# K and Q computed with tokens as rows and turned to head rows on VectorE, in place of a trip through HBM, with a new opening

## What is computed

```python
Q = (layernorm(x) @ Wq.T + bq).reshape(bs, sl, H, HD)      # H = 16, HD = 32
K = (ctx @ Wk.T + bk).reshape(bs, sl, H, HD)
V = (ctx @ Wv.T + bv).reshape(bs, sl, H, HD)
score = jnp.einsum('bshd,bsgd->bshg', Q, K)
weight = jax.nn.softmax(score, axis=-1)
attn = jnp.einsum('bshg,bsgd->bshd', weight, V).reshape(bs, sl, nf)
x = x + tanh(g_xattn[0]) * (attn @ Wo.T + bo)
x = x + tanh(g_ffn[0]) * (layernorm(x) @ (weight * scale_weight[:, None]).T + bias)
```

## Time and profile before

| | us |
|---|---|
| median of 3 runs | 281.89 |
| lowest, highest | 281.75, 282.75 |
| span of the profiled execution | 280.1 |
| TensorE busy in it | 267.5 (96%) |
| VectorE busy | 198.8 (71%) |
| ScalarE busy | 144.5 (52%) |
| GpSimd busy | 88.4 (32%) |
| DMA moved | 53.8 MB |

### The profile page before, as it was taken

How to read it: one execution, slowest core, us unless ns; L and a number is a source line. 1 busy time by engine, 2 the same in 40 slices (tenths; PEclk the granted TensorE clock), 3 DMA queues, 4 the chain that set the end, 5 groups by cost and what they waited for, 6 DMA issues and landing times.

```text
span 280.1 us, 8653 instructions
## 1 busy us (share of the span) xinstructions
PE 267.5 (96%) x3516; PEld 235.9 (84%) x3516; DVE 198.8 (71%) x331; ACT 144.5 (52%) x276; POOL 88.4 (32%) x80
## 2 busy tenths in 40 slices
PE   7899998498999999999999999999999999999995
PEld 7789997397978898888988899889988998887775
DVE  2775569189885987569774987579773855598884
ACT  4755543853686236643387225933289432954700
POOL 4104000032157116422183024612183031802722
PEclk9999999899999999999999999999999999999999
DMA  6997769991887764894488853986478729263203
GB/s 204 351 382 226 208 247 249 258 232 56 274 248 237 147 225 150 235 220 139 160 232 247 191 195 130 240 225 156 181 201 246 158 77 231 74 128 72 104 37 112
DMA packets 71912, 53.83 MB, mean 192 GB/s; under 512 B 36688, under 2 KB 59984, under 8 KB 71888
## 3 DMA queue, kind: packets, MB, share of 16 engines
q1 hardware_dynamic: 71744, 52.97, 65.6%
q10 hardware_dynamic: 144, 0.52, 0.5%
HBM read 34.08 MB, written 19.40 MB: 191 GB/s over the span
## 4 chain that ended last, share of the span: by engine, by line
PE 69%; DMA 10%; SPq 7%; ACT 7%; DVE 3%; issue 3%; DVEq 0%; ACTq 0%
PE acc L496 55%; PE score_ps L496 4%; PE score_ps L616 3%; DMA raw_spare<-wq_t 3%; ACT late L796 3%; PE attn_ps L638 3%; PE turn_ps L530 2%; DMA v_scratch<-v_or_norm 2%; SPq L350 2%; DMA k_rows<-k_scratch 2%; DMA q_pad<-q_scratch 2%; SPq L398 1%; SPq L335 1%; DVE turned L1002 1%; DMA q_scratch<-q_t 1%
## 5 line engine op out<-in xcount | busy, mean ns | idle before, releaser
L796 ACT ACTIVATE late<-attn_ps 32x256 f32<-32x256 f32 x124 | 46.6, 376 | 6.1 <-PE attn_ps L638 3.2
L496 PE MATMUL acc<-ctx_parts,wk_parts 128*128 128x256 f32 x384 | 48.7, 285 | 0.3 <-DVE late L1079 0.2
L496 PEld LDWEIGHTS acc<-ctx_parts,wk_parts 128*128 128x128 f32 x384 | 47.1, 191 | 1.7 <-issue 0.8
L1242 POOL TENSOR_TENSOR rstd<-var_eps,minus_half 128x1 f32<-128x1 f32 (+1 forms) x24 | 17.5, 728 | 95.3 <-DVE var_eps L937 95.3
L496 PE MATMUL acc<-wv_parts,ctx_parts 128*128 128x512 f32 x192 | 46.0, 394 | 0.8 <-ACT wv_parts L720 0.8
L496 PEld LDWEIGHTS acc<-wv_parts,ctx_parts 128*128 128x128 f32 x192 | 35.4, 188 | 8.1 <-issue 1.0
L496 PE MATMUL acc<-xa_parts,wq_parts 128*128 128x256 f32 x336 | 41.1, 281 | 0.1
L496 PE MATMUL acc<-wo_parts,xa_parts 128*128 128x512 f32 x168 | 40.4, 395 | 0.6 <-ACT xa_parts L720 0.6
L496 PEld LDWEIGHTS acc<-xa_parts,wq_parts 128*128 128x128 f32 x336 | 40.2, 188 | 0.7 <-DVE xa_parts L913 0.5
L496 PEld LDWEIGHTS acc<-wo_parts,xa_parts 128*128 128x128 f32 x168 | 31.0, 188 | 7.9 <-ACT xa_parts L720 1.0
L496 PE MATMUL acc<-wf_parts,x_parts 128*128 128x512 f32 (+1 forms) x132 | 29.7, 380 | 0.1
(11 more groups left out here) (89 smaller groups left out, 377.7 us busy)
## 6 DMA issues: line engine op xcount, KB each, us to landing
ctx_raw<-ctx_t SPq DMA_DIRECT2D x8, 512.0 KB, 4.7
x_norm<-x SPq DMA_DIRECT2D x8, 512.0 KB, 5.2
k_scratch<-k_t SPq DMA_DIRECT2D x8, 512.0 KB, 3.7
k_rows<-k_scratch SPq DMA_DIRECT2D x32, 128.0 KB, 3.4
q_pad<-q_scratch SPq DMA_DIRECT2D x32, 128.0 KB, 3.2
v_scratch<-v_or_norm SPq DMA_DIRECT2D x32, 128.0 KB, 2.2
v_keys<-v_scratch SPq DMA_DIRECT2D x16, 256.0 KB, 4.3
x_res<-x SPq DMA_DIRECT2D x8, 512.0 KB, 3.8
```

What stands on the lines that cost most here:

```text
L496: last = pe.matmul(dst, left(a, k), right(b, k), start=(n == 0), stop=(n == len(terms) - 1))
L796: nc.scalar.activation(attn_rows(t, q), attn_block(t, q), ACT.Identity).then_inc(a_out, 1)
L1242: nc.gpsimd.tensor_tensor(rstd[which][:, t], var_eps[which][:, t], minus_half[:, t], ALU.pow).then_inc(n_rstd[which], count)
```

## The change

K and Q become layers with tokens as rows (`rows_layer`, 24 matmuls of 512 columns each), one tile in each `acc` bank. VectorE takes each tile out with a block transpose (32x32 blocks) that gives head rows at once: `k_turn(c, t)` to `k_t`, `q_turn(c, t)` to `q_t`. It then adds the biases, `k_bias(c)` writing `k_keys` and `q_bias(c)` in place. ScalarE writes `q_pad` from `q_t` in two instructions with a scale of 0 or 1 per partition (`q_pads`). The scratch tensors of K and Q in HBM, their four kinds of DMA, `cols_bias` and `lay_keys` are gone. The biases come in as eight small DMAs.

The order of tokens in a group changes with the layout: each of the four groups of `attn_ps` now holds tokens of both tiles. `attn_high(c, 0)` therefore waits for all 16 copies, and both `attn_high` stand behind the second lot of copies. V is written to HBM in one DMA where there were four.

In `product` the order of the passes is HI·HI, LO·HI, HI·LO; before it was HI·HI, HI·LO, LO·HI, so that the low part of the left operand is now needed after 4 matmuls and not after 8.

In the opening the context and Wk come in smaller pieces split by feature block, `first_layer` runs K(0), V(0) and Q(0) piece by piece over both tiles, into `acc`, `attn_ps` and `score_ps`; the warm-up has 8 matmuls (`WARM`), before it had 12; the context of chunk 1 has a buffer of its own (`spare_parts`); the transposes of x for chunk 2 stand in step 1 and not at the end of step 0.

On the last chunk the copies are split between ScalarE and VectorE by group, with half as many columns each (`last_attn_copy`).

```diff
-V_SAVED = 4 * DMA
-WARM = (12,)
+V_SAVED = DMA
+WARM = (8,)
...
+                terms = [(k, a, b) for a, b in ((HI, HI), (LO, HI), (HI, LO)) for k in range(KC)]
...
+            def q_layer(c, prev="k", prev_c=None):
+                pe.wait_ge(x1_lo, TILES * (c + 1))
+                rows_layer(x1_parts(c), "wq", q_mm, lambda t: bank_free(prev, c if prev_c is None else prev_c, t))
...
-            k_layer(0, None, 0)
-            v_layer(0, "k", lambda: turn_x1(0, lambda t: None))
-            q_layer(0, "v", 0, WQ)
-            k_layer(1, "q", 0, (0,))
+            first_k_layer()
+            first_layer(WV, ctx_parts, v_mm, lambda t: v_bank(0, t))
+            turn_x1(0, lambda t: None)
+            first_q_layer()
+            k_layer(1, "k", 0, (0,))
             turn_x1(1, x1_read(0))
-            k_layer(1, "q", 0, (1,))
-            q_layer(1, blocks=(0,))
+            k_layer(1, "k", 0, (1,))
...
                 elif first(i - 1):
                     k_layer(2, "v", 1)
+                    turn_x1(2, x1_read(1))
...
-                if first(i):
-                    turn_x1(i + 2, x1_read(i + 1))
...
+                for slot in range(PAD):
+                    nc.scalar.activation(q_pad[:, slot], q_t[:], ACT.Identity, scale=own_slot[:, slot:slot + 1]
+                                         ).then_inc(q_padded, 1)
...
-                    act.wait_ge(a_out, MOVES * c + MOVES // TILES * (tile + 1))
+                    act.wait_ge(a_out, MOVES * (c + 1))
...
-                else:
-                    x1_high(i + 1)
-                    k_bias(i + 1)
+                x1_high(i + 1)
...
-                    q_bias(i + 1)
-                attn_copy(i, 0)
+                attn_copy(i, (0, 1))
                 x2_high(i - 1)
-                attn_high(i, 0)
-                lay_keys(i + 1)
+                q_pads(i + 1)
                 if exists(i + 2):
                     ctx_high(i + 2)
-                attn_copy(i, 1)
+                attn_copy(i, (2, 3))
+                attn_high(i, 0)
                 attn_high(i, 1)
...
+            def k_turn(c, t):
+                dve.wait_ge(k_mm, TILES * c + t + 1)
+                nc.vector.transpose(k_t[:, :, HD * t:HD * (t + 1)], acc[t][:].rearrange("p (h d) -> p h d", d=HD)
+                                    ).then_inc(k_turned, 1)
...
+                nc.vector.tensor_tensor(
+                    k_keys[:], k_t[:].rearrange("p g (n s) -> p n g s", s=2),
+                    bk_keys[:].unsqueeze(1).unsqueeze(3).broadcast_to([P, GT // 2, H, 2]), ALU.add).then_inc(k_laid, 1)
...
+                nc.vector.tensor_tensor(q_t[:], q_t[:], bq_heads[:].unsqueeze(3).broadcast_to([P, QH, KC, GT]),
+                                        ALU.add).then_inc(q_biased, 1)
...
                 spread_first(i)
+                k_turn(i + 1, 1)
+                second_stats(i - 1, 0)
+                k_bias(i + 1)
+                q_turn(i + 1, 0)
+                second_apply(i - 1, 0)
+                second_stats(i - 1, 1)
...
+                second_apply(i - 1, 1)
+                q_turn(i + 1, 1)
+                q_bias(i + 1)
...
+                v_bias(i + 1, 0)
                 turned_lo(x2_parts, x2_hi, x2_lo, i - 1)
-                v_bias(i + 1, 0)
+                attn_low(i, 0)
                 v_bias(i + 1, 1)
-                attn_low(i, 0)
                 f_residual(i - 1, 0)
                 f_residual(i - 1, 1)
                 attn_low(i, 1)
```

511 lines of the change are left out of this document (247 added, 264 removed).

## The result

The changed kernel takes 319.44 us (median of 4 runs, 315.25 to 322.16), the kernel before 282.16 on the same chip (4 runs, 281.75 to 282.75). The ratio is 1.121 with a 95% interval of 1.115 to 1.127: clearly slower. (The ratio rests on the two shorter runs; what is known of why two are longer by 5 us is told with d4.) The profiled execution is the shortest, 315.25 us, with a span of 313.2. The forecast was 299.7 with a range of 290 to 310: right in direction and in the wait that it named, too small in size.

The account below looks back on a forecast made before the run. TensorE, busy 96% of the span, was taken as the bound. Opening -7.6, step 1 +4.75, loop +17.2, step 6 -0.9, end +3.0 and clock +1.3 sum to +17.8: span 297.9, time 299.7 us, range 290 to 310.

Parts of the forecast that it names:

- the wait that it named: Loop, TensorE: F's second tile waits some 3.7 us for v_bias(i+1, 1), through a 6.5 us chain from V's end.
- The clock: Half speed behind the loop's waits: one fall at 1.3 us in the sum, bounds none and one each step, 5.4.
- in the loop no wait for a DMA stands on TensorE's path: Loop: the claim by which removing the scratch traffic, a third of the DMA bytes, was said to bring nothing.
- The opening: Before score(1): waits of 4.16 and 0.92 us go, score(1) starts at 45.8, -7.6 us; bounds -5.1 and -9.
- step 1: From score(1) to score(2): 39.2 us for 34.45, +4.75, from moved transposes and VectorE's added work, with no clock fall.
- 36.4: Length of a loop step in us, score to score; four make 145.6 against 128.4 before, +17.2.
- rival (a): Loop: the clock falls in every step, giving 303.8 us; chance 0.18.
- T+21.0 for the norm: VectorE, loop: the second norm's second application is done 21.0 us after the step's score starts; TensorE wants it at T+20.1.
- k_bias: VectorE: adding K's bias takes 1.15 us, upper bound 2.06, which would raise the sum by 4 x 0.9 us.
- Rival (b): Loop: VectorE is the bound, k_bias at 2.06 and additions slowed beside GpSimd, 305 to 312 us; chance 0.12.
- Steps 6 to 8: Program's end: step 6 -0.9 us, at 26.1; then +3.0 from late norm, late transposes and 16 half-size copies at 4.8.
- rival (c): Loop: the chain behind V's end is hidden and TensorE waits for nothing, 277.6 us; chance 0.05.

Follow-up runs that it names:

- d4: Changed kernel with 10 small matmuls in step 1's 2.6 us wait ahead of V(2)'s second tile on TensorE; 317.2 us.
- a1: Changed kernel with v_bias(i+1, 1) put back ahead of attn_low(i, 0) on VectorE; 307.1 us, ratio 1.091.
- e1: Changed kernel with 12 small matmuls in the wait between F's tiles and save_y(i-1) ahead of load_v(i+1) on SyncE; 311.6 us, ratio 1.105.
- d1: b3 with the loop's context low part on VectorE, f_residual(i-1, 0) ahead of attn_low(i, 0), and step 1 and last-chunk edits; 281.8 us, ratio 1.0046.
- b3: b2 with more reordering on VectorE and SyncE in the loop, and in step 1 and the opening; 294.4 us, ratio 1.045.
- a3: Changed kernel with 12 small matmuls keeping TensorE at work in the wait between the two tiles of F; 315.5 us.
- a4: Changed kernel with save_y(i-1) moved between save_v(i+1) and load_v(i+1) on SyncE; 318.7 us (2 runs).
- c1: Kernel before, with only attn_high(i, 0) moved later on ScalarE and attn_low(i, 0) put ahead of v_bias(i+1, 1) on VectorE; 310.1 us, ratio 1.101.
- b2: b1 with one more wait on GpSimd: x2_bias(i-1) starts only when x1_apply(i+2) is done; 293.6 us, ratio 1.042.
- a2: Changed kernel with ScalarE's second lot of copies and both high parts ahead of ctx_high(i+2); 309.5 us.
- d2: b2 with whole copies on the last chunk (12 on ScalarE, 4 on VectorE) and v_bias(7, 0) ahead of attn_low(6, 0); 293.5 us.
- d3: b2 with the passes of product in their old order, HI*HI, HI*LO, LO*HI; 292.8 us.
- b1: Changed kernel with v_bias(i+1, 1) ahead of attn_low(i, 0) and save_y(i-1) ahead of load_v(i+1); 295.1 us, ratio 1.046.

## Why the prediction was wrong in size

The wait and its chain were right; three terms of the sum were not. The clock was priced as one fall at 1.3 us in the loop and cost 4.6 there. SyncE's queue was put at nothing, by the sentence that no wait for a DMA stands on TensorE's path, and cost 2.6. The opening and step 1 were sized too small, by 6.9 together. The parts in turn:

**The loop (7.3 of the 15.3 us).** One step that failed is the sentence that "in the loop no wait for a DMA stands on TensorE's path", so that SyncE's queue was left out of the sum. It holds for the kernel before. But the change also moved `save_y` behind `load_v`, past a wait for V in HBM, and the instruction list of SyncE was not priced: 2.6 us in steps 2 and 3, and in a1 a second loop of waits of 37.4 us. The larger step is the clock: one fall was in the sum at 1.3; the profile has a half-speed stretch in four of the five steps from 1 to 5, and in the three of them that are in the loop F's second tile takes 1.2 to 1.6 us more, 4.6 with the slower scores behind it. The last 1.4 are what e1's steps have over 36.4: 2.91 us from the start of F's second tile to the next score for 2.75, and a first step of 36.93. So rival (a), 303.8 with 0.18, was the true one as to the clock, and its reason against (3.7 is shorter than 4.16) was wrong: waits of 3.2 were enough, mostly. The first loop of waits itself, 6.5 us behind V's end, T+21.0 for the norm, F's second tile at T+33.7 (measured T+33.8), came out as worked out. e1, with both causes taken out, has steps of 36.7 for the 36.4 of the forecast.

**VectorE's share.** k_bias was put at 1.15 by the nearest row and measured at 1.23; the upper bound came from ScalarE's `lay_keys`, which isn't the same regrouping: it reads every element alone, k_bias two at a time. The Trainium skill ("SBUF — State Buffer", section "Door 1: The DMA port swizzle") asks for two hits on a line of 16 bytes for full bandwidth, and k_bias makes two, so the page doesn't put it near the upper bound, as the prediction has it. The trace agrees with the page: 1.23 us for 1024 elements read eight bytes at a time is no more than the 1.22 of a low part read in a row. Rival (b), VectorE as the bound, is refuted by d1. Its mechanism, instructions slowed beside GpSimd, is real: q_bias 2.24 for 1.22. It costs where the next thing is wanted: 2.1 us in the long form of step 1, 0.8 in b3's steps, but nothing for the 0.33 that F's first tile waits.

**The opening (3.8).** Q(0) ended at 26.46 for the forecast 25.1: two waits of 0.74 and 0.77 us for the parts of x1. "VectorE, through with its queue of step 0 at about 44 (q_bias, k_bias), just keeps up" failed: k_bias(1) ends at 48.3. V(1) waits 1.12 and 0.20 us for `q_turn(1, ·)`, and score(1) 0.49 for `q_pad`. Half of that lateness is one row, the low part of Wo's second half beside GpSimd's `ctx_low(2)`:

```profile
30.52 1.18 DVE L852 TENSOR_TENSOR wo_parts<-spread,wo_parts 128x1024 fp32r<-128x1024 f32 x1
...
34.55 3.38 DVE L852 TENSOR_TENSOR wo_parts<-spread,wo_parts 128x1024 fp32r<-128x1024 f32 x1
```

It takes 3.38 us where the first half took 1.18. GpSimd's `ctx_low(2)` runs from 34.45 to 36.85. b3 moves the low part away from it and `q_bias(1)` ahead of spread, and score(1) comes at 47.3, 2.3 us earlier; no run separates the two moves. The rest is Q(0).

**Step 1 (3.1).** The forecast's 39.2 came from a timetable that the prediction doesn't show; the terms that it names add to 38.3, or 39.6 with the 1.3 for the chain. It puts V's end some 9.3 us before the next score, at T+29.9; it was at 82.2, T+32.6. The added transposes and additions were priced, but V's second tile waits 2.59 us for `q_turn(2, 1)`, later in VectorE's queue than my timetable had it, and 0.85 us are a gap inside score(1) that no row of before shows. "The clock has no reason to fall" was wrong too, though in this run it cost little: F's first tile ran at half speed while its second had to wait for the chain anyway. In the profiled runs of a3, a4 and e1, with the fall one tile earlier, step 1 is 5 us longer, and that is likely most of what lies between the profiled 315.25 and the median of 319.44.

**Steps 6 to 8 (1.2).** Step 6 as forecast, 26.2. Behind it +4.1 for +3.0: waits are where the prediction has them, O(6) 0.59 (it waits for `v_bias(7, 0)`, which stands behind the 16 copies), the transposes of chunk 6 0.57, O(7) 0.84 + 1.51 where 0.57 stood, 2.9 us together; the other 1.2 are a second wait of the transposes, 0.29, and gaps that I can't name. The 16 copies took 5.1 us (forecast 4.8).

**The bounds.** The range ended at 310 because it took the clock from none to one fall a step at 1.3 and no second chain at all. With the clock at its upper bound the sum was 303.8. The 15.6 us from there to the median are the opening 3.8, step 1 3.1, steps 6 to 8 1.1, the rest of the loop 3.2, and the 4.4 between the profiled execution and the median. Two small slips of the prediction change nothing: four falls at 1.3 are 5.2 and not 5.4, and "faster" and "same" have 0.06 together where rival (c), from which they come, has 0.05.

## What to carry to other kernels

A wait that the change adds hides other chains of nearly the same length, and removing it alone then gives back little: list every loop of waits through a step, SyncE's queue among them, and compare their lengths with the step, not only the one that ends last. When an instruction waits for a DMA (`load_v` for `save_v`), all that is moved behind it on its queue is late by the transfer's time, whether or not it has to do with it. And price a wait of some 3 us on TensorE with the half-speed stretch behind it, since it mostly comes: of the waits of 2.9 to 4.8 us in loop steps of the changed kernel, a1, a4, c1 and d4, 18 of 19 had it.

## What the runs showed of the hardware

- **VectorE and GpSimd hold each other up.** An addition, a subtraction or an application of the norm, with all inputs in SBUF, takes its own time and most of what GpSimd's instruction has left: 0.69 becomes 2.45 and 2.83, 1.18 becomes 3.38, 1.22 becomes 2.24. GpSimd loses too where the two take turns, 3.53 us for the two additions of `x2_bias` in the changed kernel, 2.55 in b2, where VectorE reads PSUM meanwhile. VectorE's instructions that read PSUM are not touched beside a busy GpSimd: 0.68 for `v_bias`, 1.27 for two low parts of `x2`, 1.31 for two transposes of the scores, as elsewhere. The Trainium skill ("SBUF — State Buffer", section "Who interferes with whom") says that only the port pair shared by these two contends, and as an exclusive lock; the rows agree.
- **The clock behind waits of like length.** Behind waits of 3.17 to 3.22 us of F's second tile in the changed kernel the tile took 3.00 once and 4.18 to 4.59 three times; behind V's wait of 2.57 to 2.60 us in step 1 it fell in seven of the ten profiles that have this wait (a2, a3, a4, b2, d2, d3, e1), and in the other three (the changed kernel, a1, b1) behind the next wait, of 2.4. Behind waits of 0.95 to 1.0 (a2's second tiles of F) it never did. But behind O(7)'s waits of 0.82 and 1.36 the layer's last 20 matmuls took 6.43 us in b2, with the clock at 0.50, and 4.84 in the changed kernel. The stretch of b2:

```profile
275.00:276.00 1.00, 1.00 (x3) 0.78 (x3) 0.00 (x0) 0.00 (x0) 0.00 (x0) 0.50 0.50 186
```

- **A gap inside score(1)** of 0.77 to 1.95 us behind the 41st of its 128 matmuls, waiting for nothing that the profile shows (51.13 above, "issue"), in every kernel with the new opening, and in none of the other scores. It grew when score(1) came earlier (b3). Its cause was not looked into.
